# First bias carried as a row of the expert weights, expert numbers read in two register loads, and bookkeeping moved to other points of the program

## What is computed

```python
logits = einsum('btd,de->bte', x, Wg) + bg
top2_vals, top2_idx = top_k(logits, 2)
scores = softmax(top2_vals)
h = einsum('btd,edh->bteh', x, W1) + b1      # 8 experts, 128 -> 512
h = gelu(h)
y = einsum('bteh,ehd->bted', h, W2) + b2     # 512 -> 128
out = sum over the two chosen experts of scores * y
ffn(x) = layer_norm(x + out) * gamma + beta

x = x + 0.5 * ffn(layernorm(x))
x = x + attention(layernorm(x))              # 16 heads of 8, 256 tokens a batch
x = x + 0.5 * ffn(layernorm(x))
```

## Time and profile before

| | |
|---|---|
| median of 3 runs | 523.98 us (517.37 to 526.24) |
| the profiled execution | 522.66 us, of which its span is 520.9 us |
| PE busy | 402.2 us (77%) |
| DVE busy | 356.2 us (68%) |
| ACT busy | 257.7 us (49%) |
| POOL busy | 213.8 us (41%) |
| blocks of the first layer (first to last `up`) | 54 to 176 us |
| attention | about 181 to 370 us |
| blocks of the second layer (first to last `up`) | 370 to 491 us |

### The profile page before, as it was taken

The page is one execution under the profiler, slowest core; times in us unless marked ns, Lnnn a source line. Parts: engine busy times, 40 slices in busy tenths (PEclk is TensorE's granted clock), DMA queues, the critical chain, the costliest instruction groups (busy, mean ns, idle before and its releaser), DMA issues. The chain is left out here.

```text
span 520.9 us, 10055 instructions
## 1 busy us (share of the span) xinstructions
PE 402.2 (77%) x3128; PEld 329.4 (63%) x3128; DVE 356.2 (68%) x1148; ACT 257.7 (49%) x515; POOL 213.8 (41%) x268
## 2 busy tenths in 40 slices
PE   1451589999899976878888878796987989999810
PEld 1441378887798855656665656554576877888710
DVE  4898124646776858999999999784364654466846
ACT  2521145755556443766566565745644356555400
POOL 4488744573544301220223243142145557335522
PEclk9999969999999965999989898977898799999965
DMA  9612621113111017960000000001112121133231
GB/s 277 231 36 72 187 58 47 47 52 92 42 47 32 23 50 238 300 197 22 7 26 4 20 11 13 10 23 41 27 37 56 38 56 47 48 92 87 67 96 41
DMA packets 32690, 37.69 MB, mean 72 GB/s; under 512 B 4992, under 2 KB 27520, under 8 KB 32240
## 3 DMA queue, kind: packets, MB, share of 16 engines
q1 hardware_dynamic: 27632, 27.32, 17.9%
q0 software_dynamic: 4544, 9.35, 5.4%
q10 hardware_dynamic: 464, 0.38, 0.4%
HBM read 26.64 MB, written 20.36 MB: 90 GB/s over the span
## 5 line engine op out<-in xcount | busy, mean ns | idle before, releaser
L1157 ACT ACTIVATE stage<-ps 128x512 f32<-128x512 f32 x78 | 46.6, 597 | 95.4 <-PE ps L722 87.0
L1729 DVE TENSOR_REDUCE mx<-ps 128x4 f32<-128x1024 f32 x64 | 77.3, 1215 | 10.5 <-PE ps L834 10.1
L1619 DVE TENSOR_TENSOR ring_hi<-ps,ring_hi 128x512 fp32r<-128x512 f32 x78 | 53.9, 691 | 39.4 <-ACT ring_hi L1164 26.6
L1211 ACT ACTIVATE stage<-ps 128x1024 f32<-128x1024 f32 x64 | 65.4, 1022 | 28.6 <-PE ps L845 27.9
L745 PE MATMUL ps<-w_hl,ring_hi 128*128 x234 | 67.0, 354 | 0.8 <-DVE stage L1627 0.8
L1613 DVE TENSOR_TENSOR bx<-ps,bx 128x128 fp32r<-128x128 f32 x78 | 22.4, 287 | 64.9 <-ACT bx L1139 54.0
L499 POOL DMA_INDIRECT expert_y<-stage x39 | 38.9, 997 | 62.1 <-DVE stage L1627 61.9
L746 PE MATMUL ps<-w_hl,ring_hi 128*128 x312 | 62.1, 240 | 0.0
L499 POOL DMA_INDIRECT expert_y<-stage,arena x39 | 38.9, 998 | 55.9 <-DVE stage L1627 53.2
L480 POOL DMA_INDIRECT sorted_x<-rows,place_at x32 | 35.4, 1107 | 56.9 <-DVE place_at L1445 50.4
L746 PEld LDWEIGHTS ps<-w_hl,ring_hi 128*128 128x128 f32 x312 | 56.1, 198 | 0.0
(11 more groups left out here) (195 smaller groups left out, 1036.6 us busy)
## 6 DMA issues: line engine op xcount, KB each, us to landing
sorted_x<-fill SPq DMA_DIRECT2D x8, 1096.5 KB, 16.3
stage<-w SPq DMA_DIRECT2D x16, 256.0 KB, 6.8
y_got<-expert_y SPq DMA_DIRECT2D x24, 128.0 KB, 2.2
stage<-sorted_x SPq DMA_DIRECT2D x39, 64.5 KB
arena<-sorted_x SPq DMA_DIRECT2D x39, 64.5 KB
x_tok<-x SPq DMA_DIRECT2D x4, 256.0 KB, 5.3
sorted_x<-rows,place_at POOLq DMA_INDIRECT x64
stage<-sel SPq DMA_DIRECT2D x1, 1024.0 KB
```

The lines of the kernel that those rows point to most:

```text
L1157: act.activation(g_full[:, s, :], ps[:, H_BANK, :], ACT.Gelu).then_inc(g_done, 1)
L1211: act.activation(prob[:, 2 * v:2 * v + 2, :], ps[:, at:at + 2, :], ACT.Exp, scale=SCALE)\
L1619: vec.tensor_tensor(bg_lo[:, s, :, :].rearrange("p c n -> p (c n)"), ps[:, G_BANK, :], bg_hi[:, s, :, :].rearrange("p c n -> p (c n)").bit ...
L1729: vec.tensor_reduce(mx[:, t, :].rearrange("p (r g j) -> p r j g", r=2, g=2)[:, pair, 2 * jp:2 * jp + 2, :], ps[:, at:at + 2, :].rearrange( ...
```

## The change

- **b1 as a weight row.** Because the features of a row sum to zero, feature 0 is minus the sum of the others. `rows1` has 130 numbers now, of which 129 are scattered as before. `up` has three matmuls and doesn't wait for `picked`; `down` waits for it.
- The subtraction is a matmul of each expert's W1 by a constant matrix (`fold_w`), plain float32, 512 columns, on PE in the head, into PSUM banks 0 to 3. `split_high` and `split_low` read W1 from PSUM. b1 is split by ACT and DVE, and SP writes its 16 rows to partition 127 of `w1_hi` and `w1_lo`, a DMA of 2 KB each.
- **Expert numbers** are read by two loads for each layer: 9 and 30 registers, 13 and 26.
- **Other points.** `placing(3)`, `rank_blocks(1)` and `list_blocks(1)` on DVE come behind `rows_low(0)` and `rows_low(1)`; `second_rows(3)`, `(4)` and `(7)` on ACT move; the splits of the weights on ACT stand in another order.

```diff
@@ PE
+            def fold_w(e):
+                pe.wait_ge(b_loaded, 48)
+                pe.wait_ge(w_loaded[e], 32)
+                if e >= 4:
+                    pe.wait_ge(w_split, e - 3)
+                pe.matmul(ps[:, e % 4, :], fold, w_raw[:, 0, e, :], start=True, stop=True).then_inc(w_folded, 1)
...
-                pe.wait_ge(picked, n + 1)
                 pe.wait_ge(bx_lo_done, n + 1)
-                pe.matmul(o, pick_r[:, n % PB, :], b_rows[:, 0:HID], start=True, stop=False)
-                pe.matmul(o, bx_hi, hi, start=False, stop=False)
+                pe.matmul(o, bx_hi, hi, start=True, stop=False)
                 pe.matmul(o, bx_hi, lo, start=False, stop=False)
                 pe.matmul(o, bx_lo, hi, start=False, stop=True).then_inc(h_filled, 1)
...
-                    pe.load(expert_regs[third:third + many], expert_of[0:1, i:i + many])
+                def load_experts(part):
+                    first, many = table_slots(TABLES * phase + part)
+                    pe.wait_ge(sched_ready, TABLES * phase + part + 1)
+                    pe.load(expert_regs[first:first + many], expert_of[0:1, first:first + many])
...
-                    if s + 1 < SLOTS and s + 1 == slot_group(phase, s + 1)[0]:
-                        load_experts(s + 1)
+                    if s + 1 == EARLY[phase]:
+                        load_experts(1)
@@ ACT
-                act.activation(w1_hi[:, e, :], w_raw[:, 0, e, :], ACT.Copy).then_inc(w_hi_done, 1)
+                act.wait_ge(w_folded, e + 1)
+                act.activation(w1_hi[0:P - 1, e, :], ps[0:P - 1, e % 4, :], ACT.Copy).then_inc(w_hi_done, 1)
@@ DVE
-                vec.tensor_tensor(w1_lo[:, e, :], w_raw[:, 0, e, :], w1_hi[:, e, :].bitcast(F32), ALU.subtract)
+                vec.tensor_tensor(w1_lo[0:P - 1, e, :], ps[0:P - 1, e % 4, :], w1_hi[0:P - 1, e, :].bitcast(F32),
+                                  ALU.subtract)
@@ SP
+            for part, rows in enumerate((b1_hi, b1_lo)):
+                sp.wait_ge(b1_steps, part + 1)
+                for e in range(EXPERTS):
+                    sp.dma_start((w1_hi, w1_lo)[part][P - 1:P, e, :].bitcast(F32),
+                                 rows[e:e + 1, :].bitcast(F32)).then_inc(b1_moved, 16)
             sp.wait_ge(w_split, 3)
             table_ready(0)
```

More of the change, by code:

```diff
@@ L51 @@
 FRONT = GT - 1
[L52 removed]
+CONSTS_SET = 12
 SCHED_STEPS = (23, 20, 23, 19)
@@ L223, in build @@
         b_raw, tri_raw, base_raw = spare[:, 0:HID + D], spare[:, 640:640 + P], spare[:, 768:768 + EXPERTS]
+        fold = spare[:, 776:776 + P]
         stage = sb("stage", [P, 2 * EXPERTS * HID])
@@ L619, in _ @@
         def _(pe):
-            expert_regs = [pe.alloc_register(f"pe_expert{i}") for i in range(12)]
+            expert_regs = [pe.alloc_register(f"pe_expert{i}") for i in range(SLOTS)]
             def pass3(out_ap, wh, wl, vh, vl, start=True, stop=True):
@@ L692, in head @@
                 rank(1)
+                for e in range(4):
+                    fold_w(e)
                 transpose_x(2)
@@ L696, in head @@
                 router(3)
+                fold_w(4)
+                fold_w(5)
                 pe.wait_ge(sched, 1)
                 rank(2)
+                fold_w(6)
+                fold_w(7)
                 pe.wait_ge(rank_steps, 5)
@@ L746, in down @@
                     pe.matmul(one, bg_lo[:, s, c, :], w_hi, start=False, stop=False, skip_group_check=True)
-                pe.matmul(one, pick_r[:, n % PB, :], b_rows[:, HID:HID + D], start=False, stop=False,
+                pe.wait_ge(picked, n + 1)
+                pe.matmul(one, pick_r[:, n % PB, :], b_rows[:, :], start=False, stop=False,
                           skip_group_check=True)
@@ L754, in blocks @@
                 n0 = phase * SLOTS
[L755 to L768 removed]
+                experts = {}
+                def load_experts(part):
+                    first, many = table_slots(TABLES * phase + part)
+                    pe.wait_ge(sched_ready, TABLES * phase + part + 1)
+                    pe.load(expert_regs[first:first + many], expert_of[0:1, first:first + many])
+                    for i in range(first, first + many):
+                        experts[i] = pe.snap(expert_regs[i], min_val=0, max_val=EXPERTS - 1)
                 load_experts(0)
@@ L772, in blocks @@
                     if s == 0 and phase == 0:
+                        pe.wait_ge(w_split, 5)
                         turn_rows(n0)
@@ L1108, in second_rows @@
                 act.wait_ge(ids_set, q + 2)
-                act.activation(rows2[:, q % 3, :, 0:D], rows1[:, 2 * r:2 * r + 2, 0:D], ACT.Copy)\
+                act.activation(rows2[:, q % 3, :, 0:D], rows1[:, 2 * r:2 * r + 2, 1:1 + D], ACT.Copy)\
                     .then_inc(rows2_done, 1)
@@ L1123, in head @@
                 second_rows(2)
-                for e in range(6):
+                act.wait_ge(b_loaded, 48)
+                act.activation(b1_hi, b_raw[0:EXPERTS, 0:HID], ACT.Copy).then_inc(b1_steps, 1)
+                for e in range(4):
                     split_high(e)
+                second_rows(3)
                 copy_x(2)
+                copy_x(3)
+                split_high(4)
+                second_rows(4)
+                split_high(5)
                 split_high(6)
-                copy_x(3)
                 split_high(7)
-                second_rows(3)
-                second_rows(4)
                 second_rows(5)
@@ L1171, in blocks @@
                     pick(n0)
-                    second_rows(7)
                 for s in range(SLOTS + 1):
@@ L1269, in beside_first @@
             def beside_first(s):
+                if s == 1:
+                    second_rows(7)
                 if s == 9:
@@ L1606, in head @@
                 add_chosen(3)
-                placing(3)
-                rank_blocks(1)
-                list_blocks(1)
             def rows_low(n):
@@ L1633, in blocks @@
                 rows_low(n0)
+                if phase == 0:
+                    placing(3)
+                    rank_blocks(1)
                 for s in range(SLOTS + 2):
@@ L1828, in beside_first @@
             def beside_first(s):
+                if s == 0:
+                    list_blocks(1)
                 if s == 10:
```

43 lines of the change are left out of this document (20 added, 23 removed).

## The result

The changed kernel takes 532.31 us (median of 4 runs, 529.58 to 533.26) against 523.41 us for the kernel before beside it (4 runs, 517.37 to 526.24): a ratio of 1.020, 95% interval 1.010 to 1.030. It is slower; whether by more or by less than 2%, the interval leaves open. The profiled execution took 532.09 us with a span of 530.3, which is 9.4 us more than the span before.

The account below looks back on a forecast made before the run. Outside attention, a two-step loop was taken to pace the smooth steps, just above PE's own work. Gains of -17.2 us and load costs of +5.4 gave -11.8 from 522.66: 510.9, said as 511, range 503 to 525.

Parts of the forecast that it names:

- the loads: PE's loads of 30 and 26 registers: several wide reads each, 3.1 and 2.8 us, costing +5.4 us with their stalls.
- the head with the first steps: Before `up(0)`: moved tables bring it forward, folds delay it somewhat, at about 52.2 us; -2.0, between 0 and -5.
- four smaller terms: Steps outside the two smooth stretches: shorter `up` and fewer small loads give -1.5, -2.5, -1.3 and -1.5 us.
- Word by word: Rival: unaligned big loads read each word singly, 7.6 and 6.6 us, clock falls twice; 525.4 us, chance 0.32.
- The price of a stop: PE waiting behind the load of 30, +2.6 us, then half clock, +2.1; the load of 26, +0.7.
- The pace: Smooth stretches: a two-step loop through `turn_g` waiting for `g_low` sets 2.44 us a step; -4.3 and -4.1 us.
- PE's own pace: Rival: the loop gives way, smooth steps fall to about 2.32 us, clock holds behind the load; 504.7 us, chance 0.11.
- The tables: Head, DVE: with three tables moved from ahead of `rows_low(0)`, `up(0)` may come at 51.6 us instead of 54.05.
- The price of a fold: Head, PE: a fold takes between 0.86 and 2.1 us, taken as 1.7, so four fill each of PE's gaps.
- stall of 4.51 us: ACT idle ahead of 65.14 us, without a cause in the profile; may swallow part of the head's gain.
- The head gives it back: Rival: slow folds delay sorting and moved tables hold first blocks; head costs 5 us, total 518, chance 0.09.
- a wait on `picked` in `down`: Sign against the forecast: a new wait standing on `picked` in `down` would show it wrong; no size given.

## Why the prediction was wrong

I said 511 and no more than 525; it was 532.1 for the profiled execution. Two steps failed, the loads (+5.4 forecast, +14.8 measured) by 9.4 us and the head with the first steps (-2.0 forecast, +7.0 measured) by 9.0; four smaller terms make 2.4 more.

- **The loads.** The step that failed is "I take the lower by a little, because the eight words show that one load can hold several wide reads". They can, from an aligned start. From slots 9 and 13 every number is a read of its own: (7271 - 319) / 29 = 0.24 us and (6228 - 319) / 25 = 0.24 us, the 0.25 of the prediction. The rival *Word by word* had 7.6 and 6.6 us. The eight words that tipped the balance began at an aligned slot and so said nothing on this; the four from slot 9 were the nearest row, and they spoke for the rival. The Trainium skill (Runtime: NRT & Kernel Launch, "Instruction fetch mechanics") has about 200 ns for each register even in bulk, for loads from HBM where these read SBUF, and was nearer for these two loads (6.0 and 5.2 us) than my choice; for aligned groups of four the runs don't agree with it (0.33 us for four).
- **The price of a stop.** In place of +5.4 the steps with loads cost 11.16 - 2.44 = 8.7 us more than a smooth step and 10.37 - 4.28 = 6.1 more than the same step before, 14.8. The rival had 19.9, since it charged 4.3 us for the clock at each; after the first load PE was back to 0.76 us for four transposes 4.5 us after its restart, and the step cost 8.7 - 7.3 = 1.4 more than the load.
- **The pace.** Right. 39.20 us for 16 steps where 39.0 stood, -3.9 where -4.1 stood, and the wait of `turn_g` 0.15 us behind `g_low` in nearly every step. From 84.77 to 137.97, 17 steps without that of the load take 42.0 us, 2.47 each, against 2.44. PE's own pace, 2.32, is out. The four smaller terms came out at -0.8, -2.0, -0.8 and -0.8 for -1.5, -2.5, -1.3 and -1.5: 4.4 us in all where 6.8 stood (the prediction miscounted the steps: the first of these stretches has six, not five, that from 144.57 has nine to the last `up`, not eleven, and that from 370.45 has 13 with the load's, not 12).
- **The head.** The step that failed is "`rank(3)` and `turn_rows(0)` end up to 2 us later: `up(0)` at about 52.2"; it came at 59.62. "-2.0, between 0 and -5" was +5.6, and the five steps behind it +1.5. The tables were right (51.57 for 51.6). The price of a fold was right, 5.46 / 4 = 1.37 us for 1.7. What failed is the sum of the two: with the folds in place the first `up` comes 7.1 us later than without (58.58 and 51.46). On a chip without pauses it comes at 48.2 to 49.3 in a kernel with all folds, 0.6 to 1.8 us before that of the kernel without folds (49.9, with the tables moved too but ACT and DVE in the order of before), so what costs is not PE's time by itself. The prediction noted a stall of 4.51 us without a cause and said it might "swallow part"; it took it for one event of the trace, where it is a kind of idle time that another arrangement of the same head meets at other places. *The head gives it back* (+5, chance 0.09) had the size, by another cause.
- Nothing was found of a wait on `picked` in `down`, and SP's 16 DMAs were issued by 27.3 us, long before DVE had done the three splits that SP waits for next (37.4 us); that they make pauses longer is neither shown nor excluded.
- **The range.** It ended at 525, and *Word by word* had 525.4: half of a rival with a chance of 0.32 stood outside the range that was to hold it.

**What stays open** is the cause of the pauses. Shown is that they come with the chip or the time at which it was used (each chip was used once), that in the head ACT and DVE go on at the same moment, and that a head with all folds loses more by them: 7.7 to 8.8 us against 0.2 to 1.6 in heads without, by the first `up` of the same kernel, or the same head, on the two kinds of chip.

## What to carry to other kernels

Begin register loads at a multiple of four words and keep them in full fours: an aligned four (0.33 us) costs as much as one word (0.32) and hides behind queued matmuls, while a long load from slot 9 or 13 takes 0.24 us a word, in which PE does nothing else. Where two readings of a row compete, ask which row has the very condition of the case (here the start of the load), and not which is more frequent. An unexplained stall in a trace is a risk for every arrangement of that stretch: it belongs into the range, and where the gain of a change is some ten microseconds, a second profile on another chip is worth having. Two kernels that are to be compared belong into one comparison: 0.966 for a kernel and 0.990 for its parent, read in different comparisons, were 0.990 for each side by side.

## What the runs showed of the hardware

- A register load reads four words at once only if the whole load begins aligned: 31 words 2.72 us, 27 words 2.35, four 0.33. A remainder goes word by word (three aligned words 0.78 us), and from a start one word behind a multiple of four all of it does (30 words 7.27 us, 26 words 6.23, four about 1.05). The last three words of the second layer took 1.07 to 1.42 us in 12 of 13 profiles, which this doesn't explain.
- The same kernel took 505.0 and 504.4 us on two chips and 522.9 to 524.7 on three. Most of the difference lies in the first blocks of each mixture layer (16.0 us), about half as idle time of PE behind pauses that nothing in the profile names, half as PE work at a lower granted clock (0.85 and 0.89 against 1.00); in a kernel with folds there is more in the head.
- After a stop of 7.3 us four transposes took 1.06 us where they take 0.63, and 0.76 us 4.5 us after the restart; the step with the stop had a mean granted clock of 0.62, the 34.80 us behind it 0.97.
